# Gating biases as one weight row: a constant last channel in place of a bias product and a three-part split

## The chip, the core and the metric

The kernel runs on one core of a Trainium2 chip. The metric is the device time of one execution in microseconds (us), here the median of several runs. The core's engines work side by side and meet only at semaphores: TensorE (PE in the rows, its weight loads PEld) multiplies and transposes, VectorE (DVE) and ScalarE (ACT) do the elementwise work, GpSimd (POOL) prepares constants and small things, and SyncE (SP) issues most of the DMAs. TensorE reads its operands from SBUF and writes to PSUM; DVE and ACT bring results back to SBUF.

## What is computed

One layer of a perceiver: a sparse linear cross attention of 4 x 256 query rows over 4 x 4096 context rows, a gated running sum, and a feed-forward part with simulated four-bit quantisation, each added to `x`. The change touches the middle one alone:

```python
def _L0_attn_ref(x, W_qkv, b_qkv, W_gate, b_gate):
    qkv = jnp.einsum('bsd,ed->bse', x, W_qkv) + b_qkv
    q, k, v = jnp.split(qkv, 3, axis=-1)
    kv_state = jnp.cumsum(k * v, axis=1)
    g = jax.nn.sigmoid(jnp.einsum('bsd,ed->bse', x, W_gate) + b_gate)
    return q * kv_state * g

x = x + _L0_xattn_ref(_layernorm(x, axis=-1), ctx_1024, ctx_1024, ...)
x = x + _L0_attn_ref(_layernorm(x, axis=-1), W_qkv, b_qkv, W_gate, b_gate)
x = x + _L0_ffn_ref(_layernorm(x, axis=-1), ...)
```

The layer norm has no learned scale or shift, so the 256 channels of a normalised row sum to zero. The biases are not zero (normal noise of 0.1).

## The kernel before

The work has three stretches. **At the start** the weights are loaded and transposed, and the queries and the first context rows are projected. **The middle** is a pipeline over 16 groups of 1024 context rows, three groups deep: TensorE projects a group, ACT takes it out of PSUM, logarithms and exponentials follow, and DVE finds in a sorting network which entries of each head survive. **The tail** is a hand-written order on each engine: the attention output is finished, then come the eight tiles of the gated running sum (`gate_tile(0)` to `gate_tile(7)`, 128 rows each), the transposes of the feed-forward weights between them, and last the feed-forward part in four chunks. Every engine runs its own list strictly in order; what stands in the list, and the semaphores, set all timing.

The weights of the stage that the change touches are `W_qkv` and `W_gate`, together 1024 rows of 256. They land in rows 8 to 15 of `w_rows` (semaphore `w_rest_loaded`, which counts `Wv` and `Wp` as well). TensorE transposes all weights in "quads" of four 128x128 blocks: quads 0 and 1 for `Wq` and `Wk`, then, after the projection of the first context group, quads 2 and 3 for `Wv` and `Wp` and quads 4 to 7 for the 1024 rows. Quad q of the last four reads rows 2q and 2q+1 of `w_rows`. There are two PSUM banks for quads, so a quad waits until ACT has copied out the one before the last. ACT's copies of quads 4 to 7 fill `WattT` (L422, the line of all quad copies). In ACT's list they stand ahead of everything of the next group, the exponentials of the queries (L500) among it.

In the tail, a gate tile is two halves (`gate_half`), each of 512 output columns: two fp32 products over the two halves of the channels (L905; the trace records each as two instructions, so four rows a half), and then a bias product (L907): three rows of ones in bf16 times three rows of bf16 bias parts. ACT reads a finished tile (sigmoid L611, copy of k L614), and DVE takes k times v and q times g from it (L1330, L1332). `running(t)` on TensorE makes the running sum of one tile, and DVE adds it (`run`, L1317, L1318).

The three parts of the biases are made on GpSimd once, after its cross-partition maximum (L389): rounding to bf16, subtracting, rounding again (L403, L405), and three DMAs that lay the parts out as rows (L408). TensorE waits for those before gate tile 0.

The normalised rows of this stage are `x_hat2`, a part of `focus_words`. ACT writes them (`normalise`, L453), and TensorE transposes them (`xhat2_quad`).

Of the kernel before, what the change touches and what calls it, by code (L numbers as in the profile page):

```python
# [35 lines left out]
PAIRS = T // 2  # L36
# [27 lines left out]
def perceiver_layer(nc, x, ctx, Wq, Wk, Wv, Wp, focus, W_qkv, b_qkv, W_gate, b_gate,  # L64
# [3 lines left out]
    def sb(name, shape, dt=F32):  # L68
        return es.enter_context(nc.sbuf_tensor(name, shape, dt))

    def sem(name):
        return es.enter_context(nc.semaphore(name))

    with es:
# [53 lines left out]
        ones_b = sb("ones_b", [3, P], BF16)  # L128
        bias_col = sb("bias_col", [P, 4 * D // P])
        bias_left = sb("bias_left", [P, 2, 4 * D // P])  # L130
        bias_parts = sb("bias_parts", [3, 4 * D], BF16)
        bias_split = sb("bias_split", [P, 3, 4 * D // P], BF16)
# [74 lines left out]
        bias_steps = sem("bias_steps")  # L207
        bias_parts_ready = sem("bias_parts_ready")
# [84 lines left out]
        def tail_quad(name):  # L293
            return AFTER_QUAD + TAIL_QUADS.index(name)
# [63 lines left out]
        def _(pool):  # L358
            pool.dma_start(in_scale[:, 0:1], s_in.rearrange("(a b) -> a b", a=1).broadcast_to([P, 1])).then_inc(small_loaded, 16)
            pool.dma_start(in_scale[:, 1:2], s_in_down.rearrange("(a b) -> a b", a=1).broadcast_to([P, 1])).then_inc(small_loaded, 16)  # L360
            at = 0
            for b in (b_qkv, b_gate):
                n = b.shape[0] // (4 * D // P)
                pool.dma_start(bias_col[at:at + n, :], b.rearrange("(p c) -> p c", p=n)).then_inc(small_loaded, 16)
                at += n
# [18 lines left out]
            pool.memset(ones_b[:, :], 1.0).then_inc(consts_ready, 1)  # L384
            for s in range(PER_BATCH):
                pool.memset(ctx_ring[:, s, :, D:GW], 1.0).then_inc(consts_ready, 1)

# [5 lines left out]
            pool.wait_ge(small_loaded, 64)  # L393

            def bias_step(ins):
                ins.then_inc(bias_steps, 1)
                bias_done[0] += 1
                pool.wait_ge(bias_steps, bias_done[0])

            bias_done = [0]  # L400
            rest = bias_col[:, :]
            for part in range(3):
                bias_step(pool.tensor_copy(bias_split[:, part, :], rest))  # L403
                if part < 2:
                    bias_step(pool.tensor_tensor(bias_left[:, part, :], rest, bias_split[:, part, :], ALU.subtract))  # L405
                    rest = bias_left[:, part, :]
            for part in range(3):
                pool.dma_start(bias_parts[part:part + 1, :].rearrange("a (p c) -> a p c", p=P),  # L408
                               bias_split[:, part, :]).then_inc(bias_parts_ready, 16)

        @block.scalar
        def _(act):
# [36 lines left out]
            def normalise(k, dst):  # L449

                act.wait_ge(norm_ready, k)
                for t in range(T)[NORM_TILES[k]]:
                    act.activation(dst[:, t, :], xs[:, t, :], ACT.Identity, scale=rstd[:, t:t + 1],  # L453
                                   bias=shift_ln[:, t:t + 1]).then_inc(x_hat_ready, 1)
# [200 lines left out]
            normalise(1, x_hat2)  # L655
# [17 lines left out]
            normalise(2, x_hat2)  # L673
# [49 lines left out]
        def _(pe):  # L723
            pe.wait_ge(consts_ready, 10)
            pe.wait_ge(w_loaded, 32)

            def transpose_quad(q, blocks):
                if q >= 2:

                    pe.wait_ge(quad_in_sbuf, q - 1)  # L730
                par = q % 2
                for b, src in enumerate(blocks):
                    ins = pe.transpose(quad_bank[par][:, b * P:(b + 1) * P], src, ident[:, :])  # L733
                ins.then_inc(quad_in_psum, 1)
# [5 lines left out]
            def two_tiles(rows, m):  # L740

                return [rows[:, t, k * P:(k + 1) * P] for t in (2 * m, 2 * m + 1) for k in range(KT)]
# [37 lines left out]
            for q in range(QK_QUADS, W_QUADS):  # L780
                transpose_quad(q + 2 * PAIRS, two_tiles(w_rows, q))
# [99 lines left out]
            def xhat2_quad(m):  # L881
                pe.wait_ge(x_hat_ready, T + 2 * m + 2)
                transpose_quad(tail_quad(f"xhat{m}"), two_tiles(x_hat2, m))
# [13 lines left out]
            def gate_half(t, half):  # L897

                if half == 0:
                    pe.wait_ge(quad_in_sbuf, tail_quad(f"xhat{t // 2}") + 1)  # L900
                    if t >= 2:
                        pe.wait_ge(gate_read, t - 1)
                dst = bank[2 + 2 * (t % 2) + half][:, :]
                for k in range(KT):
                    pe.matmul(dst, TAIL_ROWS[f"xhat{t // 2}"][:, 2 * (t % 2) + k, :],  # L905
                              WattT[:, k, half * 512:(half + 1) * 512], start=(k == 0), stop=False)
                ins = pe.matmul(dst, ones_b[:, :], bias_parts[:, half * 512:(half + 1) * 512], start=False, stop=True)  # L907
                if half == 1:
                    ins.then_inc(qkvg_in_psum, 1)
# [63 lines left out]
            pe.wait_ge(bias_parts_ready, 48)  # L973
# [49 lines left out]
        def _(dve):  # L1023
# [115 lines left out]
            dve.wait_ge(consts_ready, 10)  # L1139
# [207 lines left out]
            def weight_scales():  # L1347

                dve.wait_ge(small_loaded, 64)
# [200 lines left out]
```

## Time and profile before

| What | Value |
|---|---|
| Median of 3 runs | 500.61 us (499.62 to 500.88) |
| The profiled execution, device time | 500.58 us |
| Its span, first to last instruction | 498.8 us |
| Mean granted TensorE clock, share of full speed | 0.921 |
| Busy: DVE, PE, ACT, POOL | 451.6, 394.2, 359.9, 16.0 us |

The profiled execution lies within 0.03 us of the median, and 1.8 us of its device time lie outside the span. Busy time is summed over the whole execution; which engine holds up the end differs from stretch to stretch, so the tables by stretch, the chain of work that ended last and the waits say more than the sums. Times of rows count from the start of the span. A PE duration is a modelled one and overlaps its successor; the distance from one start to the next is the better measure.

### The profile page before, as it was taken

The numbers are of one execution on the slowest core, as the hardware profiler recorded it, in microseconds if no ns is written. First come the engines' busy times: TensorE is split into PE (matmuls) and PEld (weight loads), VectorE is DVE, ScalarE is ACT, GpSimd is POOL, SyncE is SP. The second block draws the span as 40 slices with busy tenths as digits, with TensorE's granted clock in tenths as the row PEclk, the third lists the DMA queues.
The fourth block names the chain that finished last, engine by engine and source line by source line (L and its number), as shares of the span: only waits on it lengthen the run. The fifth ranks groups of instructions, "written<-read, shape, count | busy, mean of one in ns | idle before, by whom it ended". The sixth has DMA issues, their size and how long they took to land.

```text
span 498.8 us, 6006 instructions
## 1 busy us (share of the span) xinstructions
PE 394.2 (79%) x1877; PEld 306.2 (61%) x1880; DVE 451.6 (91%) x772; ACT 359.9 (72%) x941; POOL 16.0 (3%) x32
## 2 busy tenths in 40 slices
PE   1997739999979879879879898548999897565664
PEld 1876638888868768768768787437864344123233
DVE  4698999999999999999999999999888557889983
ACT  2569697999979879879879789645277666556642
POOL 4002420000000000000000000000000000000000
PEclk9998978999999999999999899789899999668757
DMA  7942000122112112112112022022000000000001
GB/s 237 360 162 85 1 1 29 57 84 87 39 46 85 42 44 85 41 45 86 40 45 84 2 85 84 2 84 84 2 0 0 1 1 0 2 0 1 22 21 42
DMA packets 27102, 27.65 MB, mean 55 GB/s; under 512 B 1216, under 2 KB 26816, under 8 KB 27072
## 3 DMA queue, kind: packets, MB, share of 16 engines
q1 hardware_dynamic: 26704, 27.27, 16.7%
q8 instruction: 15, 0.25, 0.2%
q14 instruction: 15, 0.12, 0.1%
q0 software_dynamic: 224, 0.01, 0.0%
q10 hardware_dynamic: 144, 0.00, 0.0%
HBM read 26.22 MB, written 1.05 MB: 55 GB/s over the span
## 4 chain that ended last, share of the span: by engine, by line
DVE 66%; PE 19%; ACT 9%; issue 4%; DMA 1%; SPq 0%; ACTq 0%
DVE focus_words L1179 6%; DVE mask L1237 6%; PE bank L765 6%; DVE focus_words L1165 6%; PE bank L905 4%; DVE sorted L1195 3%; DVE merge L1213 3%; DVE sorted L1196 3%; DVE level L1188 3%; DVE level L1189 3%; ACT focus_words L500 3%; DVE sorted L1109 3%; PE bank L733 2%; DVE amax L1078 2%; PE bank L942 2%
## 5 line engine op out<-in xcount | busy, mean ns | idle before, releaser
L765 PE MATMUL bank<-WkT,rows_T 128*128 128x256 f32 x512 | 124.2, 392 | 24.0 <-ACT rows_T L422 24.0
L871 PE MATMUL bank<-ctx_words,focus_words 128*128 128x257 f32 x512 | 120.4, 395 | 27.9 <-ACT focus_words L511 27.8
L871 PEld LDWEIGHTS bank<-ctx_words,focus_words 128*128 128x128 f32 x512 | 102.5, 203 | 42.6 <-ACT focus_words L511 30.6
L765 PEld LDWEIGHTS bank<-WkT,rows_T 128*128 128x128 f32 x512 | 97.3, 196 | 40.5 <-ACT rows_T L422 28.1
L500 ACT ACTIVATE focus_words<-focus_words,shift,ff 128x256 f32<-128x256 f32 x136 | 79.8, 588 | 0.6
L511 ACT ACTIVATE focus_words<-focus_words,row_scale 128x256 f32<-128x256 f32 x136 | 56.2, 503 | 33.1 <-DVE row_scale L1181 33.1
L422 ACT ACTIVATE rows_T<-bank 128x512 f32<-128x512 f32 x78 | 43.4, 599 | 20.6 <-PE bank L733 20.6
L467 ACT ACTIVATE focus_words<-bank 128x256 f32<-128x256 f32 x136 | 50.3, 385 | 6.8 <-PE bank L765 5.5
L1165 DVE SCALAR_TENSOR_TENSOR focus_words<-focus_words,key_and,key_xor 128x2048 int32<-128x2048 int32 x17 | 39.9, 2345 | 2.2 <-ACT focus_words L467 2.2
L1237 DVE TENSOR_TENSOR mask<-focus_words,fifth 128x2048 bf16<-128x2048 f32 x17 | 38.8, 2284 | 0.1
L1179 DVE TENSOR_TENSOR focus_words<-focus_words,mask 128x2048 f32<-128x2048 f32 x17 | 38.1, 2241 | 0.0
L484 ACT ACTIVATE focus_words<-focus_words 128x2048 f32<-128x2048 f32 x17 | 32.6, 1918 | 7.5 <-DVE focus_words L1165 7.2
L733 PE MATMUL bank<-ident,ctx_words 128*128 128x128 f32 x256 | 36.4, 275 | 0.6 <-PE bank L788 0.3
L733 PEld LDWEIGHTS bank<-ident,ctx_words 128*128 128x128 f32 x256 | 31.2, 143 | 5.9 <-issue 1.2
L905 PE MATMUL bank<-WattT,rows_T 128*128 128x512 f32 x64 | 30.8, 604 | 0.0
L942 PE MATMUL bank<-gateT,focus_words 128*128 128x512 bf16 x30 | 15.0, 592 | 19.0 <-DVE ctx_words L1323 8.7
L467 ACT ACTIVATION_READ_ACCUMULATOR focus_words<-bank 128x1 f32 x136 | 28.4, 209 | 0.0
L500 ACT ACTIVATION_READ_ACCUMULATOR focus_words<-focus_words,shift,ff 128x1 f32 x136 | 25.4, 187 | 0.0
L733 PE MATMUL bank<-ident,focus_words 128*128 128x128 f32 x80 | 14.0, 316 | 12.8 <-DMA focus_words<-in_L_xattn_Wk_dram 9.7
L1188 DVE TENSOR_TENSOR level<-focus_words 128x1024 f32<-128x1024 f32 x17 | 20.7, 1218 | 0.1
L1195 DVE TENSOR_TENSOR sorted<-level 128x1024 f32<-128x1024 f32 x17 | 20.7, 1217 | 0.1
L1189 DVE TENSOR_TENSOR level<-focus_words 128x1024 f32<-128x1024 f32 x17 | 20.7, 1216 | 0.0
(188 smaller groups left out, 592.6 us busy)
## 6 DMA issues: line engine op xcount, KB each, us to landing
ctx_words<-in_ctx_dram SPq DMA_DIRECT2D x32, 512.0 KB, 3.7
ctx_words<-in_L_ffn_gate_w_dram SPq DMA_DIRECT2D x2, 1024.0 KB, 7.6
ctx_words<-in_L_ffn_up_w_dram SPq DMA_DIRECT2D x2, 1024.0 KB, 8.6
xs<-in_x_dram SPq DMA_DIRECT2D x4, 256.0 KB, 5.0
ctx_words<-in_L_ffn_down_w_dram SPq DMA_DIRECT2D x2, 512.0 KB, 9.5
ctx_words<-in_L_ffn_down_w_dram SPq DMA_DIRECT2D x1, 1024.0 KB, 4.8
out_dram<-xs SPq DMA_DIRECT2D x4, 256.0 KB, 2.1
focus_words<-in_L_attn_W_qkv_dram SPq DMA_DIRECT2D x1, 768.0 KB, 8.3
```

Of the source, the lines that this page charges most:

```text
L422: ins = act.activation(dst, src, ACT.Copy)
L467: ins = act.activation(lifted[(s + 1) % 2][:, t, :], proj_bank[m][:, (t % 2) * D:(t % 2 + 1) * D], ACT.Prelu, bias=NOT_ZERO, alpha=-0.01, ...
L500: ins = act.activation(expo[slot][:, t, :], lifted[slot][:, t, :], ACT.Exp, bias=shift[:, t:t + 1], scale=ff[:, 0:1], accum_out=exp_sum[:, ...
L511: ins = act.activation(expo[slot][:, t, :], expo[slot][:, t, :], ACT.Identity, scale=row_scale[:, slot, t:t + 1])
L733: ins = pe.transpose(quad_bank[par][:, b * P:(b + 1) * P], src, ident[:, :])
L765: ins = pe.matmul(proj_bank[m][:, t * D:(t + 1) * D], rows_T[:, m % 2, 2 * t + k, :], WT[:, k, :], start=(k == 0), stop=(k == KT - 1))
L871: ins = pe.matmul(sum_bank[k][:, 0:GW], heads_half(expo[slot][:, t, :], k), ctx_ring[:, s, t, :], start=(s == 0 and t == 0), stop=(s == PE ...
L905: pe.matmul(dst, TAIL_ROWS[f"xhat{t // 2}"][:, 2 * (t % 2) + k, :], WattT[:, k, half * 512:(half + 1) * 512], start=(k == 0), stop=False)
L1165: dve.scalar_tensor_tensor(out=key[n % 2].bitcast(I32), in0=lifted[(s + 1) % 2].bitcast(I32), scalar=key_and[:, 0:1], in1=key_xor[:, :].re ...
L1179: tt(expo[slot], expo[slot], mask[:, :, :], ALU.mult).then_inc(masked_ready, 1)
L1188: step(tt(level1[:, :, 0:4:2, :], k4[:, :, 0:4:2, :], k4[:, :, 1:4:2, :], ALU.min))
L1237: step(tt(mask[:, :, :].rearrange("p t (j h) -> p t j h", h=HEADS), key[n % 2].rearrange("p t (j h) -> p t j h", h=HEADS), fifth[:, :, :]. ...
```

## The change

The constant-times-bias product is left out. In its place the last channel of `x_hat2` is the constant 1, and the last weight row (channel 255) is the bias. What channel 255 gave before is taken over by the others: as a normalised row sums to zero, its last entry is minus the sum of the rest, so the weight of channel 255 is subtracted from the other 255 weights of each output row.

- GpSimd waits for the weights and subtracts column 255 from columns 0 to 254 in place, row block by row block (eight instructions of 128x255 fp32). TensorE waits for two of them before each of quads 4 to 7.
- After the quads have been copied, GpSimd loads `b_qkv` and `b_gate` over partition 127 of the second half of `WattT` (two DMAs). They wait behind the cross-partition maximum in its list.
- After the last exponentials of the context, GpSimd sets column 255 of `x_hat2` to 1. ACT writes 255 columns instead of 256 there.
- The bias parts, their casts and subtractions, five DMAs on GpSimd (two loads and three of the parts; two loads come in their place), and the 16 bias products are gone.

```diff
@@ block.gpsimd
-            at = 0
-            for b in (b_qkv, b_gate):
-                n = b.shape[0] // (4 * D // P)
-                pool.dma_start(bias_col[at:at + n, :], b.rearrange("(p c) -> p c", p=n)).then_inc(small_loaded, 16)
-                at += n
...
-            pool.memset(ones_b[:, :], 1.0).then_inc(consts_ready, 1)
             for s in range(PER_BATCH):
                 pool.memset(ctx_ring[:, s, :, D:GW], 1.0).then_inc(consts_ready, 1)
+
+            pool.wait_ge(w_rest_loaded, 64)
+            for r in range(8, 16):
+                pool.tensor_scalar(w_rows[:, r, 0:D - 1], w_rows[:, r, 0:D - 1], w_rows[:, r, D - 1:D], None, ALU.subtract)\
+                    .then_inc(last_taken_off, 1)
 
             pool.wait_ge(absmax_ready, 1)
             pool.partition_all_reduce(w_absmax_all[:, :], w_absmax[:, :], P, bass.bass_isa.ReduceOp.max)\
                 .then_inc(absmax_reduced, 1)
 
-            pool.wait_ge(small_loaded, 64)
...
-            bias_done = [0]
-            rest = bias_col[:, :]
-            for part in range(3):
-                bias_step(pool.tensor_copy(bias_split[:, part, :], rest))
-                if part < 2:
-                    bias_step(pool.tensor_tensor(bias_left[:, part, :], rest, bias_split[:, part, :], ALU.subtract))
-                    rest = bias_left[:, part, :]
-            for part in range(3):
-                pool.dma_start(bias_parts[part:part + 1, :].rearrange("a (p c) -> a p c", p=P),
-                               bias_split[:, part, :]).then_inc(bias_parts_ready, 16)
+            pool.wait_ge(quad_in_sbuf, W_QUADS + 2 * PAIRS)
+            at = 0
+            for b in (b_qkv, b_gate):
+                n = b.shape[0]
+                pool.dma_start(WattT[P - 1:P, KT - 1, at:at + n], b.rearrange("(a c) -> a c", a=1))\
+                    .then_inc(bias_row_loaded, 16)
+                at += n
+
+            pool.wait_ge(expo_ready, CGROUPS + 1)
+            pool.memset(x_hat2[:, :, D - 1:D], 1.0).then_inc(ones_in_last, 1)
@@ block.scalar
-            def normalise(k, dst):
+            def normalise(k, dst, cols=D):
...
-            normalise(1, x_hat2)
+            normalise(1, x_hat2, D - 1)
...
-            normalise(2, x_hat2)
+            normalise(2, x_hat2, D - 1)
@@ block.tensor
             for q in range(QK_QUADS, W_QUADS):
+                if q >= 4:
+                    pe.wait_ge(last_taken_off, 2 * q - 6)
                 transpose_quad(q + 2 * PAIRS, two_tiles(w_rows, q))
...
             def xhat2_quad(m):
                 pe.wait_ge(x_hat_ready, T + 2 * m + 2)
+                if m == 0:
+                    pe.wait_ge(ones_in_last, 1)
...
                 for k in range(KT):
-                    pe.matmul(dst, TAIL_ROWS[f"xhat{t // 2}"][:, 2 * (t % 2) + k, :],
-                              WattT[:, k, half * 512:(half + 1) * 512], start=(k == 0), stop=False)
-                ins = pe.matmul(dst, ones_b[:, :], bias_parts[:, half * 512:(half + 1) * 512], start=False, stop=True)
+                    ins = pe.matmul(dst, TAIL_ROWS[f"xhat{t // 2}"][:, 2 * (t % 2) + k, :],
+                                    WattT[:, k, half * 512:(half + 1) * 512], start=(k == 0), stop=(k == KT - 1))
...
-            pe.wait_ge(bias_parts_ready, 48)
+            pe.wait_ge(bias_row_loaded, 32)
```

GpSimd's list before, from the constants (`order`, an index table) to the end. An ISA row is a change of the engine's loaded code or the reduction itself:

```order
L382 IOTA order 128x256
L384 MEMSET ones_b 3x128
L386 MEMSET ctx_words 128x8 x4
L389 ISA
L389 ISA w_absmax_all<-w_absmax 128x3
L403 CAST bias_split<-bias_col 128x8
L405 ISA
L405 TENSOR_TENSOR bias_left<-bias_col,bias_split 128x8
...
L408 DMA bias_parts<-bias_split 1x128x8 x3
```

The same place now:

```order
L373 IOTA order 128x256
L376 MEMSET ctx_words 128x8 x4
L380 TENSOR_SCALAR focus_words<-focus_words 128x255 x8
L384 ISA
L384 ISA w_absmax_all<-w_absmax 128x3
L392 DMA WattT<-in_L0_attn_b_qkv_dram 1x16x48
L392 DMA WattT<-in_L0_attn_b_gate_dram 1x16x16
L397 MEMSET focus_words 128x8
```

The eight subtractions (L380; `focus_words` holds `w_rows`) stand ahead of the maximum and of its change of code, and no change of code stands in front of them but the one for the constants; everything that used the three-part split is gone.

TensorE's list before, gate tiles 3 (second half) to 5 with what stands between (`upto` and `ones`: running sums; `ident`: transposes of `x_hat2`):

```order
L905 MATMUL bank<-WattT,rows_T 128x512 x2
L907 MATMUL bank<-bias_parts,ones_b 128x512
L895 MATMUL bank<-focus_words,upto 128x256
L733 MATMUL bank<-ident,focus_words 128x128 x4
L905 MATMUL bank<-WattT,rows_T 128x512 x2
L907 MATMUL bank<-bias_parts,ones_b 128x512
L905 MATMUL bank<-WattT,rows_T 128x512 x2
L907 MATMUL bank<-bias_parts,ones_b 128x512
L894 MATMUL bank<-focus_words,ones 128x256
L895 MATMUL bank<-focus_words,upto 128x256
```

The same place now:

```order
L897 MATMUL bank<-WattT,rows_T 128x512 x2
L887 MATMUL bank<-focus_words,upto 128x256
L721 MATMUL bank<-ident,focus_words 128x128 x4
L897 MATMUL bank<-WattT,rows_T 128x512 x4
L886 MATMUL bank<-focus_words,ones 128x256
L887 MATMUL bank<-focus_words,upto 128x256
```

Nothing changed its place on TensorE; only the bias products between the fp32 products went, so that the two halves of a tile now stand back to back.

## Rows read from the trace of the kernel before

**Rows 1.** The page's chain that ended last, its shares by engine.
```profile
DVE 66%; PE 19%; ACT 9%; issue 4%; DMA 1%; SPq 0%; ACTq 0%
```

**Rows 2.** The chain in order of time: start, us, what; 28 to 40 us.
```profile
28.25 3.46 PE bank L765 x16
...
39.18 2.49 ACT focus_words L500 x9
```

**Rows 3.** Timeline of PE, quads 4 to 7: start, us, instruction, idle before.
```profile
32.89 1.21 PE L733 MATMUL bank<-ident,focus_words 128*128 128x128 f32 x8 [0.31 <-ACT WvT L422]
...
34.29 1.21 PE L733 MATMUL bank<-ident,focus_words 128*128 128x128 f32 x8 [0.20 <-ACT WattT L422]
```

**Rows 4.** SyncE's last weight DMA in its timeline, and its landing.
```profile
17.28 2.17 SPq L331 DMA_DIRECT2D focus_words<-in_L_attn_W_gate_dram  x1
...
DMA to landing us min/median/max: 8.4/8.4/8.4
```

**Rows 5.** Timeline of POOL.
```profile
6.02 0.41 POOL L382 IOTA order<- 128x256 int32 x1
...
49.29 1.17 POOL L403 CAST bias_split<-bias_col 128x8 bf16<-128x8 f32 x1
57.71 2.98 POOL L405 TENSOR_TENSOR bias_left<-bias_col,bias_split 128x8 f32<-128x8 f32 x1 [7.25 <-issue]
...
61.09 0.25 POOL L405 TENSOR_TENSOR bias_left<-bias_left,bias_split 128x8 f32<-128x8 f32 x1
61.41 2.19 POOL L403 CAST bias_split<-bias_left 128x8 bf16<-128x8 f32 x1
```

**Rows 6.** Timeline of DVE, 25 to 64 us.
```profile
25.53 1.23 DVE L1188 TENSOR_TENSOR level<-focus_words 128x1024 f32<-128x1024 f32 x1
...
32.73 1.22 DVE L1213 TENSOR_TENSOR merge<-sorted 128x1024 f32<-128x1024 f32 x1
...
44.00 0.20 DVE L1173 RECIPROCAL rcp_sum<-exp_sum 128x8 f32<-128x8 f32 x1 [1.85 <-ACT focus_words L500]
...
49.19 1.23 DVE L1188 TENSOR_TENSOR level<-focus_words 128x1024 f32<-128x1024 f32 x1
...
61.20 2.34 DVE L1165 SCALAR_TENSOR_TENSOR focus_words<-focus_words,key_and,key_xor 128x2048 int32<-128x2048 int32 x1
```

**Rows 7.** All bias products: duration ns least/median/most, first and last start.
```profile
L907 PE MATMUL bank<-bias_parts,ones_b x16: 384/384/385, 371.3 to 417.2; 3*128 3x512 bf16 x16
```

**Rows 8.** The chain in order of time, gate tile 4.
```profile
395.87 1.72 PE bank L905 x4
397.58 0.32 PE bank L907
397.90 1.91 PE bank L905 x4
399.81 0.32 PE bank L907
```

**Rows 9.** Timeline of ACT in the gate stage: tiles 1, 5 and 6, and a quad.
```profile
379.35 0.39 ACT L611 ACTIVATE focus_words<-bank 128x256 f32<-128x256 f32 x1 [0.79 <-PE bank L907]
...
395.90 0.60 ACT L422 ACTIVATE rows_T<-bank 128x512 f32<-128x512 f32 x1 [0.41 <-PE bank L733]
...
405.49 0.38 ACT L611 ACTIVATE focus_words<-bank 128x256 f32<-128x256 f32 x1 [0.38 <-PE bank L907]
...
411.34 0.38 ACT L611 ACTIVATE focus_words<-bank 128x256 f32<-128x256 f32 x1 [1.41 <-PE bank L907]
```

**Rows 10.** Timeline of DVE in the gate stage.
```profile
380.04 0.42 DVE L1330 TENSOR_TENSOR focus_words<-bank,ctx_words 128x256 f32<-128x256 f32 x1 [1.51 <-ACT ctx_words L614]
...
398.33 0.69 DVE L1117 TENSOR_SCALAR low<-level 128x1024 int32<-128x1024 int32 x1 [0.79 <-ACT level L581]
...
412.03 0.43 DVE L1330 TENSOR_TENSOR focus_words<-bank,ctx_words 128x256 f32<-128x256 f32 x1 [3.84 <-ACT ctx_words L614]
```

**Rows 11.** One window: PE, PEld, DVE, ACT, POOL busy, granted clock, DMA.
```profile
435.00:445.00 10.00, 5.29 (x18) 1.89 (x16) 9.69 (x14) 6.11 (x7) 0.00 (x0) 0.67 0.00 0
```

More of the change, by code:

```diff
@@ L127, in perceiver_layer @@
         same_head = sb("same_head", [P, HALF_HEADS])
[L128 to L132, printed above, removed]
         ff = sb("ff", [P, 1])
@@ L206, in perceiver_layer @@
         w_rest_loaded = sem("w_rest_loaded")
-        bias_steps = sem("bias_steps")
-        bias_parts_ready = sem("bias_parts_ready")
+        last_taken_off = sem("last_taken_off")
+        bias_row_loaded = sem("bias_row_loaded")
+        ones_in_last = sem("ones_in_last")
         masked_ready = sem("masked_ready")
@@ L390, in _ @@
                 .then_inc(absmax_reduced, 1)
-            pool.wait_ge(small_loaded, 64)
[L395 to L398, printed above, removed]
-            bias_done = [0]
-            rest = bias_col[:, :]
-            for part in range(3):
-                bias_step(pool.tensor_copy(bias_split[:, part, :], rest))
-                if part < 2:
-                    bias_step(pool.tensor_tensor(bias_left[:, part, :], rest, bias_split[:, part, :], ALU.subtract))
-                    rest = bias_left[:, part, :]
-            for part in range(3):
-                pool.dma_start(bias_parts[part:part + 1, :].rearrange("a (p c) -> a p c", p=P),
-                               bias_split[:, part, :]).then_inc(bias_parts_ready, 16)
+            pool.wait_ge(quad_in_sbuf, W_QUADS + 2 * PAIRS)
[7 more added lines that the diff above has]
+            pool.memset(x_hat2[:, :, D - 1:D], 1.0).then_inc(ones_in_last, 1)
         @block.scalar
@@ L447, in rstd_guess @@
                 act.activation(rstd0[:, tiles], ln_var[:, tiles], ACT.Exp, scale=-0.5).then_inc(rstd0_ready, 1)
-            def normalise(k, dst):
+            def normalise(k, dst, cols=D):
                 act.wait_ge(norm_ready, k)
                 for t in range(T)[NORM_TILES[k]]:
-                    act.activation(dst[:, t, :], xs[:, t, :], ACT.Identity, scale=rstd[:, t:t + 1],
+                    act.activation(dst[:, t, 0:cols], xs[:, t, 0:cols], ACT.Identity, scale=rstd[:, t:t + 1],
                                    bias=shift_ln[:, t:t + 1]).then_inc(x_hat_ready, 1)
@@ L723, in _ @@
         def _(pe):
-            pe.wait_ge(consts_ready, 10)
+            pe.wait_ge(consts_ready, 9)
             pe.wait_ge(w_loaded, 32)
@@ L1138, in _ @@
             dve.tensor_scalar(ff_neg[:, :], ff[:, :], -1.0, None, ALU.mult).then_inc(ff_ready, 1)
-            dve.wait_ge(consts_ready, 10)
+            dve.wait_ge(consts_ready, 9)
             step(dve.tensor_scalar(key_and[:, :], ff[:, :], 0.0, -float(HD), ALU.not_equal, ALU.mult))
@@ L1347, in weight_scales @@
             def weight_scales():
-                dve.wait_ge(small_loaded, 64)
+                dve.wait_ge(small_loaded, 32)
                 dve.wait_ge(absmax_reduced, 1)
```

## The prediction

> **What bounds the kernel now.** I read the chain that ended last first, then the timeline of each engine in the two stretches that the change touches, and the waits there. Over the whole run two thirds of the chain lie on DVE, which in the middle is occupied without a gap [rows 1]. The change does nothing in the middle. It touches two places where DVE is not the bound. The first is the start: around 28 to 40 us the chain goes through PE's projection, then weight quads 2 to 7 in turn between PE and ACT, then ACT's exponentials [rows 2, 3]. DVE waits there, 1.85 us at 44.00 us [rows 6]. From there on the chain stays with ACT and PE until the middle begins, so a late weight quad moves the end of the kernel by as much. The second is the gate stage, 369 to 418 us. The chain runs through almost every half of a gate tile there, and ACT stands idle for PE's bias product at several tiles [rows 8, 9].
>
> **Gate stage, what is removed.** Sixteen bias products, the last starting at 417.2 us, on record with 384 ns each [rows 7]. The price that counts is the distance between starts. In the chain, tile 4 takes 1.72 + 0.32 + 1.91 + 0.32 = 4.27 us [rows 8]. What will a tile take without them? It is 8 recorded fp32 instructions of 512 columns in a row. The nearest uninterrupted series is the sixteen of 256 columns at 28.25 us, the same number of columns: 3.46 us [rows 2]. So a tile gets 0.81 us shorter on PE, not 0.64: the second half loses as well the 0.19 us by which its first product starts slower behind the bf16 product.
>
> PE is only part of the chain, though, and the gain ends where ACT is next in line. I go through the places where ACT waits for PE:
> - Tile 1. PE has gained 1.6 us by then (tiles 0 and 1). ACT had waited only 0.79 us [rows 9]; before that it was busy with conversions of the feed-forward weights that do not depend on the gate tiles. DVE behind it had waited 1.51 us and can follow [rows 10]. Gain 0.79 us. It passes down DVE's list (weight codes, running sum, attention rows, statistics) and through ACT's normalisation to the `x_hat2` quad that starts the next stretch on PE at 392 us. Tile 2 and the first half of tile 3 add nothing, for PE waits there for that normalisation.
> - Second half of tile 3: 0.32 us. It moves the transposes behind it, the ACT copy at 395.90 us that had waited 0.41 us for them, the conversion behind that, and DVE at 398.33 us, which had waited 0.79 us [rows 9, 10]. So what ACT needs for tile 5 comes 0.32 us earlier.
> - Tile 5. PE would be ready 0.32 + 2 x 0.81 = 1.94 us earlier, but ACT had waited 0.38 us only [rows 9]. Gain 0.38 us on top of 0.32.
> - Tile 6. PE would be ready 0.32 + 3 x 0.81 = 2.75 us earlier. ACT had waited 1.41 us [rows 9], and its own work comes 0.70 us earlier: 2.11 us at most, less than PE offers. DVE had waited 3.84 us for it [rows 10] and follows. From here DVE and ACT carry the chain; tile 7 had no wait on ACT, so its savings are lost.
>
> Sum: 0.79 + 0.32 + 0.38 + 1.41 = **2.90 us**. It is about half of the 6.5 us (8 x 0.81) that PE saves.
>
> Behind the gates the feed-forward part moves as a whole. TensorE runs there partly at the lower level of its clock: mean grant 0.67 between 435 and 445 us, with PE busy 5.29 us of 10 [rows 11]. If pauses fall otherwise, some products change level. I take zero for it and keep 1.4 us either way in the range.
>
> **The start, what is added.** The last of the weights is issued at 17.28 us and lands 8.4 us later, at 25.7 us [rows 4]; the other three were issued before it. TensorE begins quad 4 at 32.89 us (needs two subtractions), and quad 7 about 0.4 us after 34.29 us, at 34.7 us (needs all eight) [rows 3]. So eight GpSimd instructions have 9.0 us, 1.12 us each, and the first two have 7.2 us. The trace shows no such instruction. From below: a GpSimd pass over 128x256 took 0.41 us, eight are 3.3 us [rows 5]. From above there is a wait. A cast of 128x8, which is hardly any work, took 1.17 us at 49.29 us and 2.19 us at 61.41 us; each ended with the DVE instruction that had begun just before it, one of two inputs (49.19 us for 1.23, 61.20 us for 2.34) [rows 5, 6]. An instruction of the same size at 61.09 us took 0.25 us, between short DVE instructions. I read this as: GpSimd gets at its data when DVE's running two-input instruction is over. In the stretch in question DVE's instructions are short: from 25.53 us to the start of the one at 32.73 us nine of them, the long ones 1.23 us [rows 6]. If each subtraction has to wait for one end, the eighth gets through at about 32.2 us, the end of the eighth of them, 2.5 us ahead of quad 7. That is nearest to what I expect, so the addition is hidden and I take **zero**; its cover is the projection of the first context group. The other side of the same sharing: GpSimd may hold DVE up, by at most 8 x 0.41 = 3.3 us, of which 1.85 us fall into DVE's wait at 44.00 us; 0 to 1.4 us, taken as zero. From above, eight times the longest cast would be 17.5 us, far too late; that is the rival below.
>
> A rule of the Trainium skill speaks of this place. GPSIMD Engine Reference, section "Key points", says that the engine shares its SBUF interfaces with VectorE, and that they contend where a DVE instruction has two SBUF inputs. By that rule all eight subtractions meet contention, for DVE's instructions there are nearly all of that kind; the trace agrees at the two casts. The same page ("Instruction dispatch") gives 5.95 us for the first call to freshly loaded code; the trace has 7.25 us of idle issue ahead of GpSimd's instruction at 57.71 us [rows 5]. Were that to fall ahead of the subtractions, the eight would end 7.25 us later; the list of instructions shows no change of code there.
>
> The other additions are far from their users. The change of code for the maximum now follows the subtractions: 32.2 + 7.25 = 39.5 us, before the maximum can start (47 us), and its result is used at 352 us. The bias rows are loaded at about 50 us and needed at 369 us. The memset waits for the last exponentials and for DVE at most 2.3 us, and is needed after 367 us. The casts and DMAs removed from GpSimd had nobody waiting.
>
> **The rivals.**
> - *GpSimd is late (slower).* Mechanism: each subtraction waits for a long DVE instruction, or is itself slow, and quad 7 waits for the last; ACT's copies, its exponentials and the middle wait behind it. It decides from 1.12 us each. At 2.19 us each [rows 5] the eighth ends at 25.7 + 17.5 = 43.2 us, 8.5 us late: 500.6 - 2.9 + 8.5 = 506.2 us. For it: the two casts, and the 2.98 us at 57.71 us. Against: that one was the first behind a change of code, and the next of its kind took 0.25 us; DVE's instructions are shorter here. Chance 0.18. Its mild form, 1.17 to 1.65 us each, is 0.4 to 4.2 us late: 498.1 to 501.9 us, chance 0.12.
> - *The cover is gone sooner in the gate stage.* If ACT's and DVE's lists close up after tile 1 and only that 0.79 us arrives: 499.8 us. For it: the 0.38 us at tile 5, which shows how near ACT is. Against: ACT's 1.41 us at tile 6 behind it. Chance 0.07.
> - *All that PE saves on the chain arrives*, tiles 0, 1, 4, 5 and 6 and half of 3: 5 x 0.81 + 0.32 = 4.4 us, 496.2 us. Against: the small waits of ACT at tiles 1 and 5. Chance 0.03.
>
> **The numbers.** The forecast (subtractions hidden, 2.9 us gained) has 0.60. Sum: 500.58 for the profiled execution, which is the median to 0.03 us, less 2.90 is 497.7 us; its own range is 496.3 to 499.1. A measurement can tell about 0.3%, 1.5 us, so "same" is 499.1 to 502.1. Faster: 0.59 of the forecast, 0.03, and 0.03 of the mild form: 0.65. Same: 0.01, 0.07, and 0.09 of the mild form: 0.17. Slower: 0.18. The range 496.2 to 502.1 holds all but the strong form of the rival and a little of the forecast.
>
> **What would show it.** In the changed kernel: the eighth subtraction ending before 34.7 us, no PE wait at quads 4 to 7, and ACT's exponentials again at 39.2 us; a gate tile of 3.4 to 3.5 us on PE; ACT's waits at tiles 1 and 5 gone and no wait at tile 6; DVE's wait there near 1.7 us; the first feed-forward product 2.9 us earlier. Wrong would be: PE idle before a weight quad with GpSimd as releaser, subtractions of over 1.1 us from start to start, or a DVE sorting network visibly stretched between 26 and 37 us.

## The result: 0.46% slower, and the profile after

| What | Before | After |
|---|---|---|
| Median | 501.88 us, 12 runs (499.62 to 503.37) | 503.88 us, 12 runs (501.79 to 506.1) |
| Ratio, 95% interval | | 1.0046 (1.0028 to 1.0064): 2.3 us slower (1.4 to 3.2) |
| Profiled execution, device time | 500.58 us | 504.52 us |
| Its span | 498.8 us | 502.8 us |
| Mean granted TensorE clock | 0.921 | 0.915 |

The forecast was 497.7 us, faster. The kernel became slower, by more than its measurement is uncertain. In the profile the gate stage gained what was forecast and a little more (3.3 us); the start lost nearly twice as much (6.2 us), in a place that the prediction took as free. I go through the profile of after in the order of time.

**GpSimd's timeline.** Columns: start, us, instruction, idle time before it and what ended it. After:

```profile
3.17 0.22 POOL L361 MEMSET head_pick<- 128x128 f32 x1
13.34 0.28 POOL L364 TENSOR_SCALAR_AFFINE_SELECT ident<-ident 128x128 f32<-128x128 f32 x1 [9.94 <-issue]
...
14.81 0.21 POOL L376 MEMSET ctx_words<- 128x8 f32 x4
25.51 12.03 POOL L380 TENSOR_SCALAR focus_words<-focus_words 128x255 f32<-128x255 f32 x8 [10.49 <-DMA focus_words<-in_L_attn_W_gate_dram]
```

And the same instruction, the first of the constants, in the kernel before (a row that was not among those ahead of the prediction):

```profile
4.89 0.30 POOL L373 TENSOR_SCALAR_AFFINE_SELECT ident<-ident 128x128 f32<-128x128 f32 x1 [0.49 <-POOL head_pick L370]
```

The identity matrix that TensorE transposes with was there at 5.2 us before and is there at 13.6 us now. GpSimd stood still for 9.94 us, and the profile names no releaser for it ("issue"). TensorE's first rows, after and then before, show who paid:

```profile
15.07 1.97 PE L721 MATMUL bank<-ident,focus_words 128*128 128x128 f32 x8 [15.07 <-POOL ctx_words L376]
```
```profile
9.69 1.94 PE L733 MATMUL bank<-ident,focus_words 128*128 128x128 f32 x8 [9.69 <-DMA focus_words<-in_L_xattn_Wk_dram]
```

Before, the first weights were the last thing to arrive; now it is GpSimd's constants, 5.4 us later. The first eight projections then took 3.07 us instead of 2.39 us. This 0.7 us does not follow from the late start: in e3 and e4 below, which begin later still, the same eight took 2.01 and 1.99 us, and in e1, which begins early, 2.91 us. By the 16 projections of the second context group the whole kernel is 6.2 us late (51.43 us against 45.22 us, after and before):

```profile
51.43 5.41 PE L753 MATMUL bank<-WkT,rows_T 128*128 128x256 f32 x16 [3.06 <-ACT rows_T L410]
```
```profile
45.22 5.41 PE L765 MATMUL bank<-WkT,rows_T 128*128 128x256 f32 x16 [3.06 <-ACT rows_T L422]
```

**The subtractions.** Summary of their line in after (duration in ns, least/median/most):

```profile
L380 POOL TENSOR_SCALAR focus_words<-focus_words x8: 932/946/2506, 25.5 to 35.1; 128x255 f32<-128x255 f32 x8
```

Five of them took some 0.93 us each; up to 29.22 us DVE was idle, waiting for the late start. The last three took 2.49 us each, from 30.1 us on, beside DVE's two-input instructions. The last ends at 37.54 us. TensorE begins quad 4 at 39.06 us, with all eight done, so nothing waits [compare rows 3]: the addition is hidden, because everything that it could delay is 6 us late itself.

**The middle** brings no work of the change, yet the last mask starts 8.4 us late (350.68 us against 342.25 us). The missing 2.2 us come at one place. TensorE had stood still for 3.06 us in both kernels before these products; after, then before:

```profile
63.65 3.78 PE L753 MATMUL bank<-WkT,rows_T 128*128 128x256 f32 x8 [3.06 <-ACT rows_T L410]
```
```profile
57.44 1.99 PE L765 MATMUL bank<-WkT,rows_T 128*128 128x256 f32 x8 [3.06 <-ACT rows_T L422]
```

The windows around them (PE, PEld, DVE, ACT, POOL busy; granted clock; DMA) say why. After, then before:

```profile
58.00:68.00 10.00, 6.63 (x28) 5.41 (x29) 9.93 (x22) 5.74 (x14) 0.00 (x0) 0.72 0.01 2
68.00:78.00 10.00, 7.29 (x38) 6.20 (x36) 7.36 (x6) 7.45 (x26) 0.00 (x0) 0.94 0.00 0
```
```profile
52.00:62.00 10.00, 6.63 (x41) 5.72 (x41) 9.93 (x22) 6.13 (x15) 4.07 (x4) 1.00 0.01 2
62.00:72.00 10.00, 4.37 (x25) 3.67 (x23) 10.00 (x9) 9.77 (x31) 3.41 (x4) 0.86 0.01 1
```

After, the eight products ran at the clock's lower level (granted 0.50 from 63.65 to 67.40 us, 1.2 GHz of 2.4) and took 1.8 us longer; DVE, full in the ten microseconds that follow in before, was busy for 7.36 of 10. e5 below has the same slow products without any edit ahead of them.

**The gate stage.** A tile is 8 recorded fp32 products without a bf16 one. Timeline of PE in after, tile 4 and the running sum behind it; then ACT's reads of tiles 1, 5 and 6 with the quad copy between them [compare rows 9], and its table load ahead of tile 0:

```profile
401.84 3.60 PE L897 MATMUL bank<-WattT,rows_T 128*128 128x512 f32 x8
405.27 0.59 PE L886 MATMUL bank<-focus_words,ones 128*128 128x256 f32 x2
```
```profile
380.57 1.28 ACT L650 ACT_TABLE_LOAD   x1
...
386.01 0.39 ACT L599 ACTIVATE focus_words<-bank 128x256 f32<-128x256 f32 x1
...
402.04 0.60 ACT L410 ACTIVATE rows_T<-bank 128x512 f32<-128x512 f32 x1 [0.21 <-PE bank L721]
...
405.47 0.38 ACT L599 ACTIVATE focus_words<-bank 128x256 f32<-128x256 f32 x1 [1.04 <-PE bank L897]
...
411.27 0.38 ACT L599 ACTIVATE focus_words<-bank 128x256 f32<-128x256 f32 x1
...
415.58 0.39 ACT L599 ACTIVATE focus_words<-bank 128x256 f32<-128x256 f32 x1
```

A tile goes by in 3.43 us, start to start. ACT no longer waits at tiles 1, 5 and 6 (the row at 405.47 us is tile 4, where it still waits). In the waits of the stretch, ACT's for the gate banks (us in total, times, longest), after and then before:

```profile
ACT focus_words L599 <- PE bank L897: 2.0, 2, 1.0
```
```profile
ACT focus_words L611 <- PE bank L907: 5.8, 5, 1.9
```

The lag behind the kernel before, place by place:

| Place | Before | After | Lag |
|---|---|---|---|
| ACT's table load ahead of tile 0 | 373.02 | 380.57 | 7.55 |
| ACT reads tile 1 | 379.35 | 386.01 | 6.66 |
| ACT's quad copy behind tile 3 | 395.90 | 402.04 | 6.14 |
| ACT reads tile 5 | 405.49 | 411.27 | 5.78 |
| ACT reads tile 6 | 411.34 | 415.58 | 4.24 |
| DVE's last rows | 495.54 | 499.46 | 3.92 |

So 6.2 us of lag at the start and 2.2 us in the middle are 8.4 us; 0.9 us go between the last mask and the table load; the gates give back 3.3 us and the feed-forward part 0.3 us. That leaves the 3.9 us by which the profiled executions differ.

The 0.9 us are the clock again, this time on the other side. Five microseconds behind the last mask, before and then after (columns as above):

```profile
347.25:352.25 5.00, 4.45 (x23) 4.25 (x24) 4.09 (x21) 3.38 (x9) 0.00 (x0) 0.69 0.33 135
```
```profile
355.68:360.68 5.00, 4.25 (x33) 3.85 (x34) 4.79 (x27) 3.68 (x9) 0.00 (x0) 1.00 0.49 197
```

From the last mask to the table load it is 30.77 us in before and 29.89 us in after. It is 29.89 us in e5 below too, which has before's instructions up to the first bias product at 371 us, and 30.70 us in e8, which has no bias products but a grant of 0.70 at this place: the difference goes with the clock and not with the change.

### The profile page after: what moved, and what is told of

Read it like the earlier page. It is cut to its first block, busy times and chain, and to the rows that moved or that the text cites. A ratio compares the mean times of both kernels' runs of the same rounds, so it can differ in the third digit from the quotient of the medians.

```text
span 502.8 us, 5976 instructions
## 1 busy us (share of the span) xinstructions
PE 388.6 (77%) x1861; PEld 306.1 (61%) x1864; DVE 452.0 (90%) x772; ACT 359.3 (71%) x941; POOL 19.5 (4%) x32
## 4 chain that ended last, share of the span: by engine, by line
DVE 70%; PE 13%; ACT 11%; issue 5%; POOL 1%; POOLq 0%; ACTq 0%
DVE focus_words L1170 7%; DVE mask L1228 7%; DVE focus_words L1156 6%; PE bank L753 5%; DVE merge L1204 3%; DVE sorted L1186 3%; DVE sorted L1187 3%; DVE level L1179 3%; DVE level L1180 3%; DVE sorted L1100 3%; PE bank L721 2%; DVE amax L1069 2%; PE bank L933 2%; DVE sorted L1192 2%; DVE sorted L1191 2%
## 5 line engine op out<-in xcount | busy, mean ns | idle before, releaser
L753 PE MATMUL bank<-WkT,rows_T 128*128 128x256 f32 x512 | 125.8, 396 | 24.1 <-ACT rows_T L410 24.1
L721 PE MATMUL bank<-ident,focus_words 128*128 128x128 f32 x80 | 13.6, 308 | 20.4 <-POOL ctx_words L376 15.1
L897 PE MATMUL bank<-WattT,rows_T 128*128 128x512 f32 x64 | 29.2, 594 | 0.0
L721 PEld LDWEIGHTS bank<-ident,focus_words 128*128 128x128 f32 x80 | 10.1, 157 | 24.5 <-POOL ctx_words L376 15.1
L1179 DVE TENSOR_TENSOR level<-focus_words 128x1024 f32<-128x1024 f32 x17 | 20.9, 1227 | 0.1
```

The lines of the kernel that those rows point to most:

```text
L753: ins = pe.matmul(proj_bank[m][:, t * D:(t + 1) * D], rows_T[:, m % 2, 2 * t + k, :], WT[:, k, :], start=(k == 0), stop=(k == KT - 1))
L1179: step(tt(level1[:, :, 0:4:2, :], k4[:, :, 0:4:2, :], k4[:, :, 1:4:2, :], ALU.min))
```

## The experiments

Each ratio is to the kernel before, run beside the experiment. What needed a cause was first of all the 9.94 us. GpSimd's lists (an ISA row is a change of loaded code, or the reduction) hold this, before and after:

```
before: constants (ISA, L373) ... reduction (ISA, L389) ... split (ISA, L405)
after:  constants (ISA, L364) ... subtractions L380 ... reduction (ISA, L384), and no more
```

The trace has the first of these changes in both kernels, ahead of the same instruction (least/median/most in ns, then the start):

```profile
L373 POOLq MODIFY_POOL_CONFIG  x2: 11/14/16, 4.8 to 4.8; - x2
```
```profile
L364 POOLq MODIFY_POOL_CONFIG  x2: 11/11/11, 3.6 to 3.6; - x2
```

In before the instruction behind it starts within 0.1 us, in after 9.7 us later.

**Theory A.** The change to the constants' code costs nothing in before because that code is loaded already: the previous execution ended with it, for the bias split needed the same code again after the reduction's. In after the list ends with the reduction's code, so the next execution has to load the constants' code, with nothing to hide it. **Rival B**: the two DMAs that were taken off the start had covered a load that is always there. **Rival C**: the subtractions' instruction enlarges what is loaded. The second question was what the subtractions cost once the start is mended.

**e1_code_back.** After, with a small instruction of the constants' code behind the bias DMAs; only the memset of the last channel still follows it in GpSimd's list.

```diff
+            pool.memset(lib_pair[:, 0, :], 1.0).then_inc(lib_step, 1)
+            pool.wait_ge(lib_step, 1)
+            pool.tensor_tensor(lib_pair[:, 1, :], lib_pair[:, 0, :], lib_pair[:, 0, :], ALU.subtract).then_inc(lib_step, 1)
```

> The changed kernel, and one small GpSimd subtraction of 128x8 (nothing uses it) behind the bias DMAs, so that GpSimd's list ends with the code of index 0 loaded instead of that of the maximum (index 1). Theory A, the code that one execution leaves loaded is what the next one finds: GpSimd's first AFFINE_SELECT starts at 3.5 to 5 us instead of 13.34, PE's first transpose at 9.7 instead of 15.07, the span gets 5 to 8 us shorter than that of the changed kernel, and the time 1 to 3 us shorter than the kernel before (gates -3.3, subtractions late by 0.5 to 1.5). Rival B, two DMAs fewer ahead of the first change of code expose it: AFFINE_SELECT stays at 13.3 us. Rival C, the subtractions' opcode makes the code of index 0 longer to load: stays at 13.3 us as well.

Measured: 503.03 us (12 runs), ratio 1.0035 (1.0017 to 1.0054): 1.8 us slower than before, where 1 to 3 us faster was expected. Timeline of GpSimd:

```profile
4.04 0.30 POOL L366 TENSOR_SCALAR_AFFINE_SELECT ident<-ident 128x128 f32<-128x128 f32 x1 [0.49 <-POOL head_pick L363]
...
25.29 13.64 POOL L382 TENSOR_SCALAR focus_words<-focus_words 128x255 f32<-128x255 f32 x8 [19.55 <-DMA focus_words<-in_L_attn_W_gate_dram]
...
61.99 3.38 POOL L400 TENSOR_TENSOR lib_pair<-lib_pair 128x8 f32<-128x8 f32 x1 [6.70 <-issue]
```

An edit at the end of the list took the 9.94 us from its beginning, and TensorE began at 9.34 us. Nothing ahead of the first constant differs from after, so what differs was left there by something that ran earlier; I read it as the previous execution of the same kernel. No run executes a kernel only once, so this last step is inferred. Yet the time hardly fell, for now the second cost came up. The rows of TensorE for quads 6 and 7 and the transposes behind them:

```profile
36.82 1.11 PE L727 MATMUL bank<-ident,focus_words 128*128 128x128 f32 x4 [2.48 <-POOL focus_words L382]
38.98 1.12 PE L727 MATMUL bank<-ident,focus_words 128*128 128x128 f32 x4 [1.05 <-POOL focus_words L382]
39.89 2.14 PE L727 MATMUL bank<-ident,ctx_words 128*128 128x128 f32 x8
```

The eight subtractions took 13.64 us, 1.7 us each, and ended at 38.93 us. The transposes came at 39.89 us, before at 35.78 us: 4.1 us late. At the 16 projections of the second context group it is 4.7 us (49.89 us against 45.22 us).

**e2_before_code_left.** Before, with the two subtractions of the bias split replaced by a memset, so that its list ends with the reduction's code. The second and third part of the biases are zero there.

```diff
-                    bias_step(pool.tensor_tensor(bias_left[:, part, :], rest, bias_split[:, part, :], ALU.subtract))
+                    bias_step(pool.memset(bias_left[:, part, :], 0.0))
```

> The kernel before, with the two GpSimd subtractions of the bias split replaced by memsets to zero, so that parts two and three of the biases are left out (zero) and GpSimd's list ends with the code of index 1. Four DMAs at the start, no subtraction of weights. Theory A: AFFINE_SELECT at 14 to 15 us instead of 4.89, PE's first transpose at 16 us, 5 to 9 us slower than the kernel before. Rivals B and C: as the kernel before, 4.89 us and no change of the time.

Measured: 508.26 us (6 runs), ratio 1.014 (1.0097 to 1.0182): 7 us slower (4.9 to 9.1), for putting two memsets in the place of two subtractions of 8 columns.

```profile
14.37 0.28 POOL L373 TENSOR_SCALAR_AFFINE_SELECT ident<-ident 128x128 f32<-128x128 f32 x1 [9.94 <-issue]
```

This is theory A from the other side: the same 9.94 us, in a kernel with before's DMAs and without any of the new work. TensorE's first row stands at 16.25 us, 6.6 us later than in before.

**e3_two_dmas_kept.** After, with the two loads of `bias_col` at the start again.

> The changed kernel, with the two bias loads of the kernel before kept at the start of GpSimd's list (nothing uses them). Theory A: AFFINE_SELECT still at 13 to 15 us. Rival B: back at 4.9 us.

Measured: one run of 502.75 us. The load is still there, so B falls, as it does by e2, which has all of before's DMAs.

```profile
13.92 0.28 POOL L370 TENSOR_SCALAR_AFFINE_SELECT ident<-ident 128x128 f32<-128x128 f32 x1 [9.50 <-issue]
```

**e4_no_subtraction.** After without the eight subtractions and the waits for them; the weights keep what channel 255 should have been relieved of.

> The changed kernel without the eight subtractions of column 255 and without TensorE's waits for them (this part of the computation is left out); GpSimd's list still ends with the code of index 1. Theory A: AFFINE_SELECT still at 13.3 us. Rival C: back at 3.5 to 5 us. Span within 1 us of the changed kernel's 502.8 if the subtractions were hidden there, as I think (the eighth ended at 37.54, quad 4 began at about 39).

Measured: one run of 505.09 us. The load is there without them, so C falls. One run's time can't tell whether their absence gained anything, but the trace can: from the first products of the context to the 16 of the second group it is 21.57 us here (28.97 to 50.54 us) and 21.70 us in after (29.73 to 51.43 us). So in after the subtractions cost about 0.1 us.

```profile
13.65 0.28 POOL L364 TENSOR_SCALAR_AFFINE_SELECT ident<-ident 128x128 f32<-128x128 f32 x1 [10.26 <-issue]
```

**e5_no_bias_product.** Before with the bias products alone left out (so no bias is added in the gated running sum), which leaves the gain of the gate stage by itself.

```diff
-                ins = pe.matmul(dst, ones_b[:, :], bias_parts[:, half * 512:(half + 1) * 512], start=False, stop=True)
```

> The kernel before without the 16 bias products and with nothing else changed (the biases are left out of the result). It measures the gate stage's term by itself. Theory: 2.9 us forecast, 3.3 us read from the changed kernel's profile; a ratio near 0.994, the last exponentials at the same time as before and the end 3 to 3.5 us earlier. Rival: the clock in the feed-forward part gives part of it back, less than 1.5 us.

Measured: 497.58 us (10 runs), ratio 0.9921 (0.9893 to 0.9949), 4.0 us faster (2.6 to 5.4). Its start is before's, and it shows the slow products too (timeline of PE):

```profile
start us, us, engine line op out<-in xcount [idle before <-releaser]
57.53 3.78 PE L765 MATMUL bank<-WkT,rows_T 128*128 128x256 f32 x8 [3.06 <-ACT rows_T L422]
```

So the lower clock behind that pause comes to a kernel whose start and middle are before's, instruction by instruction. Its last mask starts at 344.49 us, 2.24 us later than in before: the whole 2.2 us, without an edit. In the profiles of this case the eight products took 1.99 us twice (before, e8), 2.6 to 2.7 us three times (e1, e3, e6) and 3.78 us six times (after, e2, e4, e5, e7, e9). The profiled execution of before, at 500.58 us, lies 1.3 us below the median of its 12 runs, and 1.0 us below that of the 27 runs beside e5 (501.61 us, 498.41 to 503.42). I therefore take the 2.2 us in the middle of after as scatter and not as a cost of the change. The sums agree within their uncertainty: by the ratio of the runs after is 2.3 us slower (1.4 to 3.2), and 6.2 us of the start less the 4.0 us (2.6 to 5.4) that e5 gains is 2.2 us. Without the 0.7 us of the first projections it would be 1.5 us, so that it meets 2.3 us so closely is luck. The part of the sum behind the middle fits as well: from the last mask to DVE's last rows it is 148.78 us in after and 148.77 us in e5, against 153.29 us in before, 0.9 us of which are the clock.

**e6_code_back_no_subtraction.** e1 without the subtractions, again with channel 255 not taken off: what the change would be worth if both costs were gone.

> The changed kernel with the small GpSimd subtraction at the end (code of index 0 left loaded) and without the eight subtractions of column 255 and their waits (left out). Theory: both costs at the start are gone, so it is 2.5 to 4 us faster than the kernel before (ratio 0.992 to 0.995); quads 4 to 7 at 32.9 to 35 us. If it is not faster, a third cost is missing in my account.

Measured: 497.37 us (12 runs), ratio 0.9933 (0.9909 to 0.9958). The forecast was a ratio of 0.992 to 0.995. Between e1 and e6 stand only the eight subtractions and TensorE's waits for them: 1.0035 less 0.9933 is 5.1 us; the spans of the profiled executions differ by 5.4 us (500.0 and 494.6). The transposes behind quad 7 stand at 35.31 us in e6, 4.6 us ahead of e1, and the 16 projections of the second group at 44.74 us, 5.15 us ahead.

**e7_weights_first.** The whole computation, e1 with the two weights of the stage loaded ahead of `Wv`, `Wp` and `down_w`, under a semaphore of their own.

```diff
-            for w in (Wq, Wk, Wv, Wp, W_qkv, W_gate):
+            for w, at in ((Wq, 0), (Wk, 2), (W_qkv, 8), (W_gate, 14), (Wv, 4), (Wp, 6)):
...
-            pool.wait_ge(w_rest_loaded, 64)
+            pool.wait_ge(w_att_loaded, 32)
```

> The whole computation: the changed kernel with the code put back at the end, and the gate stage's weights loaded ahead of Wv, Wp and the feed-forward down weights, with a semaphore of their own on which GpSimd's subtractions wait. Theory: the subtractions start near 22 us, four of them at 0.93 us each before DVE's two-input instructions begin, the rest at 1.24 us each, so the eighth ends near 31 us, ahead of quad 4 at 32.9; the time is that of the kernel without subtractions, 2.5 to 4 us faster than before. Rival: the DMAs share the bandwidth, the weights land at 24.5 us or later, and quad 7 waits still 1 to 3 us; the time is then about that of the kernel before.

Measured: 498.45 us (12 runs), ratio 0.9942 (0.992 to 0.9964), faster than both kernels. The mechanism came out only in part. The subtractions began 4.1 us earlier than in e1 but met more of DVE's work, and took 14.92 us, to 36.15 us, where 31 us was expected. The other weights of the list, `Wv` and `Wp`, come behind them now. Summary of the subtractions' line, and TensorE's row for quad 7:

```profile
L382 POOL TENSOR_SCALAR focus_words<-focus_words x8: 933/1922/2772, 21.2 to 34.6; 128x255 f32<-128x255 f32 x8
...
36.20 0.66 PE L727 MATMUL bank<-ident,focus_words 128*128 128x128 f32 x4 [1.56 <-POOL focus_words L382]
```

**e8_one_dve_subtraction** and **e9_weights_first_again** were measured side by side. e8 is e7 with one instruction on DVE in place of GpSimd's eight; e9 is e7 unchanged.

```diff
+            dve.wait_ge(w_att_loaded, 32)
+            dve.tensor_tensor(w_rows[:, 8:16, 0:D - 1], w_rows[:, 8:16, 0:D - 1],
+                              w_rows[:, 8:16, D - 1:D].broadcast_to([P, 8, D - 1]), ALU.subtract).then_inc(last_taken_off, 8)
...
-            for r in range(8, 16):
-                pool.tensor_scalar(w_rows[:, r, 0:D - 1], w_rows[:, r, 0:D - 1], w_rows[:, r, D - 1:D], None, ALU.subtract)\
-                    .then_inc(last_taken_off, 1)
```

> The whole computation. As e7_weights_first (attention weights loaded early, GpSimd ends on the constants' code), but the eight subtractions on GpSimd are one subtraction of 128x8x255 on DVE, in its list behind the maxima of the first two feed-forward weights, where e7's DVE waited 1.88 us for ACT. Theory (the subtractions on GpSimd beside DVE are what holds quads 4 to 7 back in e1 and e7): one DVE instruction of about 2.3 us at 21.1 us ends at about 23.5, PE has no wait at quads 4 to 7, the quads stand within 0.5 us of before's 32.9 and 34.3, the transposes behind them at 35.8 instead of 37.7. DVE's first keys come 0.7 us later, which its wait of 2.49 us at 44.96 takes up. So e7 less 1 to 1.9 us, near e6_code_back_no_subtraction: ratio to before 0.990 to 0.994. Rival (the subtractions cost e7 nothing on the path, its 1 us over e6 is scatter): ratio as e7's, measured again in this call. Rival on the other side: DVE's list up to the masks is the path once quads are on time, then e8 loses the 2.3 us that DVE gained in work: ratio 0.996 to 1.0.

> The same kernel as e7_weights_first, measured beside e8 so that the two share the runs of before. Expected: ratio 0.992 to 0.996 again. It tells whether a difference of 1 to 2 us between e8 and e7 is one of the kernels; in its profile the subtractions should again take over 1.2 us each beside DVE's two-input instructions.

Measured: e8 497.93 us (7 runs), ratio 0.993 (0.9905 to 0.9955); e9 498.9 us (12 runs), ratio 0.9945 (0.9928 to 0.9962). Timelines of e8, DVE and then PE:

```profile
21.33 2.28 DVE L1152 TENSOR_TENSOR focus_words<-focus_words 128x2040 f32<-128x2040 f32 x1 [0.37 <-DMA focus_words<-in_L_attn_W_gate_dram]
23.57 2.35 DVE L1160 SCALAR_TENSOR_TENSOR focus_words<-focus_words,key_and,key_xor 128x2048 int32<-128x2048 int32 x1
...
44.56 0.20 DVE L1168 RECIPROCAL rcp_sum<-exp_sum 128x8 f32<-128x8 f32 x1 [1.98 <-ACT focus_words L489]
```
```profile
33.41 1.18 PE L722 MATMUL bank<-ident,focus_words 128*128 128x128 f32 x8 [0.40 <-ACT WvT L411]
34.88 1.18 PE L722 MATMUL bank<-ident,focus_words 128*128 128x128 f32 x8 [0.29 <-ACT WattT L411]
36.34 1.18 PE L722 MATMUL bank<-ident,ctx_words 128*128 128x128 f32 x8 [0.29 <-ACT WattT L411]
```

The same work takes DVE 2.28 us in a place where it had waited for ACT (1.88 us at 22.71 us in e7), and no quad waits for it; DVE still has a wait of 1.98 us at 44.56 us. The rival that this would lengthen the kernel falls. e8's median is 1.0 us below e9's, but the intervals overlap, so I count e8 as at least as good as e7 and no more. It is within the interval of e6, which leaves the subtraction out: in this form it costs nothing that these runs can tell. e9 repeats e7's ratio and its profile: eight subtractions in 15.06 us, and 1.57 us of TensorE's wait at quad 7.

## Why the prediction was wrong

- **The step that failed** is in the part on the start: "the list of instructions shows no change of code there", and "the casts and DMAs removed from GpSimd had nobody waiting". The term was put at nothing: I compared where the two lists change code and took the one for the constants as costing the same in both. Its price in before was in the trace to be read: 0.49 us at 4.89 us, where the change of code at 57.71 us had cost 7.25 us [rows 5]. A change of code that costs nothing asks for a reason, and the reason was the third one at L405, which the change takes away. Nobody in the same execution waited for the bias split; the next execution's constants did. e1 and e2 show it from both sides. On the path it costs 5.4 us of the 6.2 us (TensorE's first row at 15.07 instead of 9.69 us), not the whole 9.94 us, since the weights' DMA had hidden the difference before; the other 0.7 us came up in the first projections, and their cause stays open.
- **The price of a subtraction** was wrong as well: I took one end of a DVE instruction for each, after the two casts. Alone it took 0.93 us, more than twice the 0.41 us of my lower bound [rows 5], whose instruction reads no tensor. Beside DVE's two-input instructions of 1.2 to 1.4 us it took 2.49 us, about two of theirs and not one. My upper bound of 2.19 us each was too low for one (the longest, in e9, took 2.91 us), though the eight together stayed under it (12.03 to 15.06 us against 17.5 us).
- **The deciding point** was right: 1.12 us each. In e1, at 1.7 us each, the end at 38.93 us is 4.2 us behind the 34.7 us that the prediction sets for quad 7 (the trace has it at 34.84 us), and the measured delay is 4.1 us. The rival that GpSimd is late, to which the prediction gave 0.30 in its two forms, is thus what e1 shows, at a price between them: the mild form ends at 1.65 us each and 1.3 us above before, and e1's runs are 1.8 us above (0.9 to 2.7). In the changed kernel itself the rival stayed hidden, covered by the other cost. "Hidden" was thus right for after, by a cover that I had not named.
- **The gate stage** was right, term by term: 0.89, 0.52, 0.36 and 1.54 us at tile 1, the copy behind tile 3, tiles 5 and 6, forecast 0.79, 0.32, 0.38 and 1.41. That is 3.3 us against 2.9 us; e5 measures 4.0 us (2.6 to 5.4) for the whole. The term of the half tile 3 was too small: the running-sum product between it and the transposes, 0.63 us in the chain before, took 0.43 us without a bf16 product ahead of it. A tile takes 3.43 us on PE, forecast 3.46 us.
- **The clock** in the feed-forward part, for which I had kept 1.4 us, gave 0.3 us in all. The clock moved 2.2 us in the middle, where I had said that nothing happens, and 0.9 us the other way behind the last mask; e5 has both, with no edit ahead of either. The forecast also stood on a low start: the profiled 500.58 us matched the median of three runs, and the medians of more runs of before are 0.6 to 1.3 us above it.
- **The range** reached to 502.1 us, and the median is 503.88 us. Its upper end rested on the subtractions alone. No case had the constants at the start in it.

## What to carry to other kernels

Read GpSimd's list as a ring: all eleven traces here fit that what its end leaves loaded is what the first instruction finds at the next execution. When an edit removes the last user of a piece of GpSimd's code, look at which code the list now ends with; an 8-column instruction of the code that the start needs, in a quiet place, brought TensorE's start forward by 5.7 us here (15.07 to 9.34 us). It waited 6.70 us for its own load, where nobody waited for GpSimd. Before work is given to GpSimd beside a DVE that is full of two-input instructions, ask whether DVE has one short wait in reach: eight instructions of 1.5 to 1.9 us each became one of 2.28 us that nobody noticed.

## What the runs showed of the hardware

- **GpSimd's start depends on the code with which its list ends.** The first AFFINE_SELECT of the constants comes after 0.49 us of idle time where the list ends with its code (before, e1, and likewise e5 to e9), after 9.94, 9.94, 9.50 and 10.26 us where it doesn't (after, e2, e3, e4). That the loaded code outlives an execution is the reading of this that no run contradicts. The same change of code later in the run, at 58 to 62 us, cost 6.70 us in e1 and 7.25 us in before. The Trainium skill, GPSIMD Engine Reference, section "Instruction dispatch", gives 5.95 us for a first call to freshly loaded code and says that no instruction in the profile shows it. The trace agrees: the change itself has a row of 11 ns (MODIFY_POOL_CONFIG), and the load behind it is only "issue". All loads here were longer than the page's figure, those at the start by about 4 us.
- **A GpSimd pass of 128x255 fp32 with a per-partition operand** took 0.93 us beside an idle DVE and 2.49 us beside back-to-back DVE instructions of two inputs (after, 30.1 to 37.5 us). DVE suffers less: its 128x2048 instruction at 29.22 us in after took 2.58 us, and 2.35 us in e4, where there are no subtractions. The same page of the Trainium skill, section "Key points", names the shared SBUF interfaces as the reason; the trace agrees that both sides slow down, and GpSimd bears nearly all of it (1.56 us on each pass, against 0.23 us on DVE's longest instruction).
- **Which products run at TensorE's lower clock differs between kernels that are the same up to there.** Eight projections behind the same pause of 3.06 us took 1.99 us at a granted clock of 1.00 (before) and 3.78 us at 0.50 (after, and e5, whose list is before's up to the gate stage), and DVE lost some 2 us with them. The two profiled executions of before and after stood on different sides of this, and behind the last mask on different sides the other way round (0.9 us), so their difference of 3.9 us holds 1.3 us of this and is more than the 2.3 us by which the runs differ.
